# Two column chunks of the composed weights change their widths: 384, 512 becomes 512, 384

## The chip, the cores and the metric

The kernel runs on one core of a Trainium2 chip. The metric is the device time of one execution in microseconds (us). Three runs of the kernel before gave 673.21, 673.73 and 673.96 us; the median is 673.73 us.

## The reference

An input x of 8 sequences by 256 tokens by 1024 features goes through four residual layers. All shapes are 1024 by 1024.

```python
x = x + x @ w_eff.T                      # layer 0: quantized weight plus lora_B @ lora_A / 2
x = x + x @ W.T + 2 * lora(gates, A, B)  # layer 1: top 2 of 8 experts, gates from the logits x @ Wr.T
x = x + x @ W2.T + b + 2 * (x @ A2[id2]) @ B2[id2]   # layer 2: an adapter for each sequence
x = x + x @ W3[id3].T                    # layer 3: a whole weight for each sequence
```

The quantized weight of layer 0 is worked out from thresholds between the codebook's values, with a scale for every group of 128 inputs.

## The kernel before, in words

Everything is computed in float32 accuracy from two float32r parts: each operand is split into a high part (a copy by ScalarE, ACT) and a low part (whole minus high, by VectorE, DVE), and `product` (L1042) issues three matmuls, L1044, L1045 and L1046, for each pair of tiles.

**First phase: the weights are composed before x is touched.** The layers are linear apart from the gates, so the kernel first forms (I + W0)(I + W1)(I + W2) and the columns of the low-rank parts with it. There are two products ("steps"), each with eight row tiles m (`chunk`, L1083). The right-hand operand of step 0 is `e_both` (W2 transposed with the identity added, then the adapters' columns), and its row tiles of the left-hand operand, from W1, pass through a ring of two buffers, `ring_hi` and `ring_lo`. The results are evacuated by ACT (L582) into `e_mid`, split again (`e1`, L636, L643) and are the right-hand operand of step 1, whose left-hand tiles come from the quantized W0; its results go back to `e_both` (`e2`, L644, L650). The columns of each product are cut in three chunks, `LEFT` in step 0 and `RIGHT` in step 1: chunk 0 is 384 wide, chunk 1 is 512, chunk 2 is 256 or 392. A chunk of one row tile is 24 matmuls (8 tiles of the inner dimension, three each) into one PSUM bank.

**Order of step 0.** `CHUNKS` (L59) begins with chunk 0 of row tiles 0 and 1, then chunk 1 of both, then chunk 2 of both; from row tile 2 on the three chunks of a tile stand together. Behind the first, third and fifth of them stand `br(0)`, `br(1)` and `br(2)` (L1070), 24 matmuls each of the same widths as `LEFT`.

**How W2 arrives.** `load_w2` (L352) loads chunk c in pieces kk of two inner tiles: pieces (c, 0) to (c, 3) for chunks 0 and 1, one piece for chunk 2. Those of chunk 0 are used in the order 2, 3, 1, 0 (`W2_ORDER`); piece 2 is issued from ACT's queue and the others from SyncE's (SP). Where an inner tile k meets its own diagonal block, the identity is added to the raw data: by GpSimd (POOL) at L479, by DVE for k = 1 at L870. `CHUNK_OF` (L43) says which chunk holds the diagonal block of tile k, and `w2_diagonals` (L337) makes the list of a piece. Only then does ACT take the high part of the piece (L558), DVE the low part (L762), and PE may use it (`wait_left`, L1063).

**One list for three engines.** `phase1_plan` (L91) writes one list of steps which ACT, DVE and POOL each walk in order, each doing what is its own. In it stand the pieces of W2, the LoRA deltas (L547), the evacuations `f`, the adapters' columns `as` (L624), the ring tiles `w1` and `w0` (L568), and the "beats", the rounds in which DVE and ACT quantize W0 (L823 to L842, L575). Each engine is blocked by the first step that isn't ready.

**Second phase.** Four groups of 512 tokens: `x3_main`, the gates, the low-rank closing, and the product with the weight of layer 3. In the first group the eight tiles m of `x3_main` read `e_both` in column blocks of 128 and wait at L1153 for the chunks of step 1.

Of the kernel before, what the change touches and what calls it, by code (L numbers as in the profile page):

```python
# [36 lines left out]
TILE_AT = [A0, A0 - R2]  # L37
A_AT, WR_AT, NOW_AT = [0, R2], [ER, R2 + ER], [ER + NE, 0]

LEFT = [(0, 384), (384, 512), (896, 256)]  # L40
RIGHT = [(0, 384), (384, 512), (896, 392)]
assert sum(LEFT[2]) == A0 and sum(RIGHT[2]) == EC
CHUNK_OF = [0, 0, 0, 1, 1, 1, 1, 2]  # L43


W2_ORDER = [(2, 3, 1, 0), (0, 1, 2, 3), (0,)]
# [90 lines left out]
def build(nc, x, cb, lang, id2, id3, w0, scale_log, lora_a, lora_bt, w1, wrt, at, bcat,  # L137
          w2t, b, las, lbs, w3t, y):
    plan = phase1_plan()
    with ExitStack() as ctx:  # L140
# [191 lines left out]
        def w2_piece(c, kk):  # L332

            c0, w = LEFT[c]
            return slice(2 * kk, KT if c == 2 else 2 * kk + 2), slice(c0, min(c0 + w, D))

        def w2_diagonals(c, kk):  # L337

            return [k for k in range(KT) if CHUNK_OF[k] == c and (c == 2 or k // 2 == kk) and k != DVE_DIAG]

# [196 lines left out]
        def _(act):  # L537
# [40 lines left out]
            def evac(n):  # L578
                step, m, c = CHUNKS[n]
                c0, w = (LEFT, RIGHT)[step][c]  # L580
                act.wait_ge(chunk_mm, n + 1)
# [8 lines left out]
            for item in plan:  # L590
# [24 lines left out]
                elif what == "br":  # L615
                    c0, w = LEFT[item[1]]
                    act.wait_ge(br_mm, item[1] + 1)
# [18 lines left out]
                elif what == "e1":  # L636
                    _, c, kk = item
                    c0, w = RIGHT[c]
                    ks, cols = slice(2 * kk, 2 * kk + 2), slice(c0, min(c0 + w, A0))
# [4 lines left out]
                elif what == "e2":  # L644
                    _, c, kk = item
                    c0, w = RIGHT[c]
                    ks, cols = slice(2 * kk, 2 * kk + 2), slice(c0, c0 + w)
# [103 lines left out]
        def _(dve):  # L751
# [101 lines left out]
            for item in plan:  # L853
# [43 lines left out]
                elif what == "br":  # L897
                    c0, w = LEFT[item[1]]
                    dve.wait_ge(br_up, item[1] + 1)
# [23 lines left out]
                elif what == "e1":  # L923
                    _, c, kk = item
                    c0, w = RIGHT[c]
                    n_e1 += 1
# [3 lines left out]
                elif what == "e2":  # L930
                    _, c, kk = item
                    c0, w = RIGHT[c]
                    n_e2 += 1
# [107 lines left out]
        def _(pe):  # L1041
            def product(out, a, b_, start, stop, **kw):  # L1042

                pe.matmul(out, a[0], b_[0], start=start, stop=False, **kw)  # L1044
                pe.matmul(out, a[0], b_[1], start=False, stop=False, **kw)  # L1045
                return pe.matmul(out, a[1], b_[0], start=False, stop=stop, **kw)  # L1046
# [23 lines left out]
            def br(c):  # L1070
                c0, w = LEFT[c]
                if c == 0:
                    pe.wait_ge(bcat_lo, 1)
                if c < 2:
                    pe.wait_ge(delta_out, BR_BANK[c] + 1)
                if c == 2:
                    pe.wait_ge(br_down, 1)
                for k in range(KT):
                    ins = product(ps[:, BR_BANK[c], 0:w], (bcat_up[:, k, :], bcat_down[:, k, :]),
                                  (e_hi[:, k, c0:c0 + w], e_lo[:, k, c0:c0 + w]), k == 0, k == KT - 1)  # L1080
                ins.then_inc(br_mm, 1)
# [71 lines left out]
            def x3_main(g, m):  # L1153

                if m < 3:
                    pe.wait_ge(y_free, KT * g + 5 + m)
                if m == 3:
                    pe.wait_ge(e2_down, 12)
                if m >= 5:
                    pe.wait_ge(x3_done, KT * g + m - 4)  # L1160
                for k in range(KT):
                    if m == 0 and k % 2 == 0:

                        pe.wait_ge(e2_down, 4 + k // 2 + 1)
                        pe.wait_ge(x_lo_done, X_CREDIT + 4 * g + k // 2 + 1)
                    cols = slice(m * P, (m + 1) * P)
                    ins = product(ps[:, m % 5, :], (e_hi[:, k, cols], e_lo[:, k, cols]),
                                  (x_hi[:, k, :], x_lo[:, k, :]), k == 0, False, skip_group_check=True)
                if m == KT - 1:
                    ins.then_inc(x_used, 1)  # L1170
# [57 lines left out]
            def group(g):  # L1228
                x3_main(g, 0)
                low_rank(g)  # L1230
                x3_main(g, 1)
                x3_main(g, 2)
                turn_h2(g)
                turn_g(g)
                x3_main(g, 3)
                h2_add(g)
                x3_main(g, 4)
                for m in range(3):
                    x3_gate(g, m)
                pe.wait_ge(h2_done, g + 1)  # L1240
                pe.wait_ge(bs_done, BS_CREDIT + 2 * (g + 1))
                for m in range(3):
                    x3_close(g, m)
                for m in range(3, 5):
                    x3_gate(g, m)
                    x3_close(g, m)
                for m in range(5, KT):
                    x3_main(g, m)
                    x3_gate(g, m)
                    x3_close(g, m)  # L1250
                y_product(g, 0)
                y_product(g, 1)
# [44 lines left out]
```

## Time and profile before

| | |
|---|---|
| median of three runs | 673.73 us |
| the profiled execution | 672.66 us |
| its span in the trace | 670.8 us |
| PE busy | 663.7 us (99%) |
| PE weight load busy | 569.2 us (85%) |
| DVE busy | 353.4 us (53%) |
| ACT busy | 279.3 us (42%) |
| POOL busy | 90.7 us (14%) |
| DMA | 67.07 MB, 100 GB/s on the mean |
| chain that ended last | PE 92%, SP queue 3%, DVE 2% |

All times of the trace are counted from the start of the span; 1.9 us of the profiled execution lie outside it. Matmuls overlap, so the distance between two starts, not the duration of one, is what a matmul costs in a row of them.

### The profile page before, as it was taken

To read this page: it belongs to the slowest core of one execution; us is meant where nothing else is said; L and a number is where in the kernel's file an instruction comes from. 1 tells how busy PE (TensorE), PEld (TensorE's weight loads), DVE (VectorE), ACT (ScalarE), POOL (GpSimd) and SP (SyncE) were. 2 spreads that over 40 slices of the span, in tenths; PEclk is the share of its full clock that TensorE was granted. 3 is DMA by queue.
4 is the path that set the end of the run, shared out by engine and by line. 5 is a ranking of instruction groups with operands and counts; after the bars stand their busy time and mean duration, and the time that the engine had idled before them with its cause. 6 is when DMAs were issued, how large, how long until landed. Compare 5 with 4: busy or idle time off the path is not lost.

```text
span 670.8 us, 9252 instructions
## 1 busy us (share of the span) xinstructions
PE 663.7 (99%) x3280; PEld 569.2 (85%) x3280; DVE 353.4 (53%) x538; ACT 279.3 (42%) x417; POOL 90.7 (14%) x120
## 2 busy tenths in 40 slices
PE   7999999999999999999999999999999999999998
PEld 7889989999999988888889888888888888888886
DVE  6799899879951374215544222661421653411453
ACT  6664664952812361204552123553121564121453
POOL 3210225005010030001220000220000221000120
PEclk9999999999999999999999999999999999999999
DMA  9652111001000503003864001777000586000372
GB/s 317 190 158 84 43 38 57 1 1 63 1 1 0 189 21 129 1 1 104 298 220 155 0 0 44 260 239 231 0 0 0 193 286 214 21 0 1 104 233 103
DMA packets 39283, 67.07 MB, mean 100 GB/s; under 512 B 3541, under 2 KB 22997, under 8 KB 39253
## 3 DMA queue, kind: packets, MB, share of 16 engines
q1 hardware_dynamic: 34500, 58.15, 26.5%
q10 hardware_dynamic: 4752, 8.52, 3.7%
q8 instruction: 18, 0.29, 0.2%
q14 instruction: 13, 0.10, 0.1%
HBM read 58.27 MB, written 8.39 MB: 99 GB/s over the span
## 4 chain that ended last, share of the span: by engine, by line
PE 92%; SPq 3%; DVE 2%; DMA 1%; issue 1%; ACT 1%; DVEq 0%; ACTq 0%
PE ps L1044 28%; PE ps L1046 28%; PE ps L1045 28%; PE ps L1147 3%; PE ps L1149 1%; PE ps L1180 1%; SPq L354 1%; DMA ids_sb<-adapter 1%; DVE tmp L833 1%; SPq L394 1%; SPq L395 0%; DVE w_w L823 0%; ACT tmp L575 0%; DVE w_w L829 0%; SPq L359 0%
## 5 line engine op out<-in xcount | busy, mean ns | idle before, releaser
L762 DVE TENSOR_TENSOR ring_lo<-raw,ring_hi 128x512 fp32r<-128x512 f32 x128 | 91.5, 730 | 82.1 <-ACT ring_hi L674 82.0
L1044 PE MATMUL ps<-e_both,ring_hi 128*128 128x384 f32 (+3 forms) x384 | 133.7, 348 | 0.8 <-DVE ring_lo L762 0.4
L1046 PE MATMUL ps<-e_both,ring_lo 128*128 128x384 f32 (+3 forms) x384 | 133.4, 347 | 0.0
L674 ACT ACTIVATE ring_hi<-raw 128x512 fp32r<-128x512 f32 x128 | 79.4, 629 | 70.2 <-PE ps L1046 66.6
L1044 PE MATMUL ps<-x_both,e_both 128*128 128x512 f32 x256 | 101.5, 397 | 0.0
L1045 PE MATMUL ps<-x_both,e_both 128*128 128x512 f32 x256 | 101.2, 395 | 0.0
L1044 PE MATMUL ps<-ring_hi,e_mid 128*128 128x512 f32 x256 | 101.0, 395 | 0.0
L1046 PE MATMUL ps<-ring_hi,e_mid 128*128 128x512 f32 x256 | 101.0, 395 | 0.0
L1045 PE MATMUL ps<-ring_lo,e_mid 128*128 128x512 f32 x256 | 101.0, 394 | 0.0
L1046 PE MATMUL ps<-x_both,e_both 128*128 128x512 f32 x256 | 101.0, 394 | 0.0
L516 POOL TENSOR_TENSOR raw<-raw,ident 128x128 f32<-128x128 f32 x64 | 43.0, 674 | 317.2 <-DMA raw<-w_t 317.2
L1044 PEld LDWEIGHTS ps<-e_both,ring_hi 128*128 128x128 f32 x384 | 72.1, 188 | 6.8 <-DVE e_both L762 0.7
L1046 PEld LDWEIGHTS ps<-e_both,ring_lo 128*128 128x128 f32 x384 | 72.1, 188 | 5.7
L1018 DVE SCALAR_TENSOR_TENSOR e_mid<-ps,bias_col,e_mid 128x512 fp32r<-128x512 f32 x32 | 22.5, 746 | 94.7 <-ACT e_mid L720 94.7
L1045 PE MATMUL ps<-e_mid,ring_hi 128*128 128x384 f32 (+2 forms) x192 | 68.5, 357 | 0.0
L1045 PE MATMUL ps<-e_both,ring_hi 128*128 128x384 f32 (+2 forms) x192 | 64.8, 337 | 0.0
L575 ACT ACTIVATE tmp<-tmp,dif 128x1024 f32<-128x1024 f32 x48 | 54.2, 1151 | 22.2 <-DVE tmp L831 18.4
L833 DVE SCALAR_TENSOR_TENSOR tmp<-w_w,thr,tmp 128x1024 f32<-128x1024 f32 x48 | 60.4, 1301 | 4.2 <-ACT tmp L575 3.8
L720 ACT ACTIVATE e_mid<-ps,bias_col 128x512 fp32r<-128x512 f32 x32 | 20.4, 690 | 96.5 <-PE ps L1180 96.5
L1046 PEld LDWEIGHTS ps<-ring_hi,e_mid 128*128 128x128 f32 x256 | 48.2, 188 | 11.3
L1046 PEld LDWEIGHTS ps<-x_both,e_both 128*128 128x128 f32 x256 | 48.1, 188 | 11.5
L1045 PEld LDWEIGHTS ps<-ring_lo,e_mid 128*128 128x128 f32 x256 | 48.2, 188 | 11.3
(152 smaller groups left out, 860.9 us busy)
## 6 DMA issues: line engine op xcount, KB each, us to landing
raw<-w_t SPq DMA_DIRECT2D x64, 512.0 KB, 3.5
xraw<-x_t SPq DMA_DIRECT2D x16, 512.0 KB, 4.6
w_w<-w SPq DMA_DIRECT2D x15, 512.0 KB, 4.0
y<-tmp ACTq DMA_DIRECT2D x30, 256.0 KB, 2.6
e_both_w<-w_t SPq DMA_DIRECT2D x5, 512.0 KB, 8.4
e_mid_w<-bs SPq DMA_DIRECT2D x24, 64.0 KB, 2.8
e_both_w<-w_t SPq DMA_DIRECT2D x3, 384.0 KB, 6.7
w_w<-w SPq DMA_DIRECT2D x2, 256.0 KB, 5.2
```

Of the source, the lines that this page charges most:

```text
L354: queue.dma_start(e_lo_w[:, ks, cols], w2t[ks.start * P:ks.stop * P, cols].rearrange("(k p) c -> p k c", p=P)).then_inc(s_w2[4 * c + kk], 16)
L516: pool.tensor_tensor(d, d, ident[:, :], ALU.add).then_inc(w3_diag, 1)
L575: act.activation(acc[i], acc[i], ACT.Identity, bias=dif[:, LEVELS - 1 - level:LEVELS - level]).then_inc(q_add, 1)
L674: act.activation(ring_hi[:, (2 * k + h) % 4, :], raw[:, k % RAW, h * 512:(h + 1) * 512], ACT.Copy).then_inc(w3_hi, 1)
L720: act.activation(x3_hi[:, m, :], ps[:, m % 5, :], ACT.Identity, bias=bias_col[:, m:m + 1]).then_inc(x3_hi_done, 1)
L762: return dve.tensor_tensor(out, whole, hi.bitcast(F32), ALU.subtract)
L833: ins = dve.scalar_tensor_tensor(out=acc[i], in0=qf, scalar=thr[:, k:k + 1], in1=acc[i], op0=ALU.is_gt, op1=ALU.mult)
L1018: dve.scalar_tensor_tensor(out=x3_lo[:, m, :], in0=ps[:, m % 5, :], scalar=bias_col[:, m:m + 1], in1=x3_hi[:, m, :].bitcast(F32), op0=ALU.add,
L1044: pe.matmul(out, a[0], b_[0], start=start, stop=False, **kw)
L1045: pe.matmul(out, a[0], b_[1], start=False, stop=False, **kw)
L1046: return pe.matmul(out, a[1], b_[0], start=False, stop=stop, **kw)
L1147: pe.matmul(ps[:, 4 + t, 0:2 * TW].rearrange("p (h c) -> p h c", h=2), x_hi[:, k, cols], e_both[:, :, k, ecols], start=k == 0, stop=False, ...
```

## The change

```diff
-LEFT = [(0, 384), (384, 512), (896, 256)]
-RIGHT = [(0, 384), (384, 512), (896, 392)]
+LEFT = [(0, 512), (512, 384), (896, 256)]
+RIGHT = [(0, 512), (512, 384), (896, 392)]
...
-CHUNK_OF = [0, 0, 0, 1, 1, 1, 1, 2]
+CHUNK_OF = [0, 0, 0, 0, 1, 1, 1, 2]
...
-                if m == 3:
+                if m == 4:
                     pe.wait_ge(e2_down, 12)
```

The first chunk of both products takes 512 columns and the second 384. The diagonal block of inner tile 3 (columns 384 to 511) is now in chunk 0, and with it its identity addition belongs to piece (0, 1). In the second phase the fourth tile of `x3_main` lies wholly in chunk 0, so that the wait for chunk 1 stands before the fifth. The number of instructions on every engine is the same.

POOL's identity additions at the opening, as one piece of the difference (`s_w2_1` is the landing of piece (0, 1), `s_w2_0` of piece (0, 0), `s_w2_5` of piece (1, 1); `e_both_w` is the float32 view of `e_both`):

```order
 L479 TENSOR_TENSOR e_both_w<-e_both_w,ident 128x128 [waits s_w2_1,lora_clear]
+L479 TENSOR_TENSOR e_both_w<-e_both_w,ident 128x128 [waits s_w2_1]
 L479 TENSOR_TENSOR e_both_w<-e_both_w,ident 128x128 [waits s_w2_0]
 L479 TENSOR_TENSOR w_w<-w_w,ident 128x128 [waits s_w1_1]
-L479 TENSOR_TENSOR e_both_w<-e_both_w,ident 128x128 [waits s_w2_5]
```

One addition moved from piece (1, 1) to piece (0, 1), ahead of that of piece (0, 0).

ACT's walk through the pieces of chunk 0, one piece of the difference (`w2_diag` counts POOL's additions):

```order
-L558 ACTIVATE e_both<-e_both_w 128x2x384 [waits s_w2_2]
-L558 ACTIVATE e_both<-e_both_w 128x2x384 [waits s_w2_3]
+L558 ACTIVATE e_both<-e_both_w 128x2x512 [waits s_w2_2]
+L558 ACTIVATE e_both<-e_both_w 128x2x512 [waits s_w2_3]
 L568 ACTIVATE ring_hi<-w_w 128x512 [waits first_diag]
-L558 ACTIVATE e_both<-e_both_w 128x2x384 [waits w2_diag,s_w2_1]
-L558 ACTIVATE e_both<-e_both_w 128x2x384 [waits w2_diag_dve,w2_diag,s_w2_0]
+L558 ACTIVATE e_both<-e_both_w 128x2x512 [waits w2_diag,s_w2_1]
+L558 ACTIVATE e_both<-e_both_w 128x2x512 [waits w2_diag_dve,w2_diag,s_w2_0]
```

The four steps keep their places; each is 1024 elements long instead of 768.

ACT's queue between the second chunk of PE and the adapters' columns, again from the difference (`chunk_mm` is PE's finished chunk, `s_as` the landing of the adapters):

```order
-L582 ACTIVATE e_mid_w<-ps 128x384 [waits chunk_mm]
+L582 ACTIVATE e_mid_w<-ps 128x512 [waits chunk_mm]
 L547 ACTIVATE raw<-ps 128x512 [waits delta_mm] x3
 L558 ACTIVATE e_both<-e_both_w 128x8x128 [waits w2_diag,s_w2_8]
 L624 ACTIVATE e_both<-w_w 128x8x128 [waits s_as]
```

The evacuation of the second chunk (chunk 0 of row tile 1) is wider and nothing else moved; what stands behind it is queued behind PE's end of that chunk.

## Rows read from the trace of the kernel before

**Rows 1.** The page: busy time and the clock granted to PE.
```profile
PE 663.7 (99%) x3280; PEld 569.2 (85%) x3280; DVE 353.4 (53%) x538; ACT 279.3 (42%) x417; POOL 90.7 (14%) x120
...
PEclk9999999999999999999999999999999999999999
```
**Rows 2.** Waits of PE, whole span: us in total, times, longest.
```profile
PE ps L1044 <- DVE ring_lo L762: 0.4, 1, 0.4
PE ps L1044 <- DVE e_both L762: 0.4, 1, 0.4
```
**Rows 3.** Timeline of PE at the opening: start us, duration us, instruction.
```profile
12.66 0.34 PE L1046 MATMUL ps<-e_both,ring_lo 128*128 128x384 f32 x1
13.37 0.45 PE L1044 MATMUL ps<-e_both,ring_hi 128*128 128x384 f32 x1 [0.37 <-DVE e_both L762]
13.65 0.34 PE L1045 MATMUL ps<-e_both,ring_hi 128*128 128x384 f32 x1
...
15.41 0.34 PE L1046 MATMUL ps<-e_both,ring_lo 128*128 128x384 f32 x1
15.80 0.45 PE L1044 MATMUL ps<-e_both,e_mid 128*128 128x384 f32 x1
...
24.30 0.39 PE L1044 MATMUL ps<-e_both,ring_hi 128*128 128x512 f32 x1
...
27.10 0.39 PE L1044 MATMUL ps<-e_both,ring_hi 128*128 128x512 f32 x1
```
**Rows 4.** Timeline of PE where row tile 2 begins.
```profile
49.29 0.28 PE L1045 MATMUL ps<-e_both,ring_hi 128*128 128x256 f32 x1
49.41 0.28 PE L1046 MATMUL ps<-e_both,ring_lo 128*128 128x256 f32 x1
50.11 0.44 PE L1044 MATMUL ps<-e_both,ring_hi 128*128 128x384 f32 x1 [0.42 <-DVE ring_lo L762]
```
**Rows 5.** Timeline of POOL: identity additions of the opening.
```profile
10.11 2.14 POOL L479 TENSOR_TENSOR e_both_w<-e_both_w,ident 128x128 f32<-128x128 f32 x2 [7.55 <-DMA e_both_w<-w_t]
...
21.77 0.46 POOL L479 TENSOR_TENSOR e_both_w<-e_both_w,ident 128x128 f32<-128x128 f32 x1 [0.74 <-DMA e_both_w<-w_t]
```
**Rows 6.** The first two of these additions: ns min/median/max.
```profile
L479 POOL TENSOR_TENSOR e_both_w<-e_both_w,ident x2: 909/1090/1271, 10.1 to 11.3; 128x128 f32<-128x128 f32 x2
```
**Rows 7.** Transfers at the opening: one window, last columns clock, DMA share, GB/s.
```profile
8.00:12.00 4.00, 4.00 (x33) 4.00 (x32) 3.45 (x6) 2.89 (x5) 1.89 (x2) 1.00 1.07 388
```
**Rows 8.** Timeline of ACT.
```profile
11.47 0.85 ACT L558 ACTIVATE e_both<-e_both_w 128x768 fp32r<-128x768 f32 x1 [0.62 <-POOL e_both_w L479]
...
24.53 0.49 ACT L582 ACTIVATE e_mid_w<-ps 128x384 f32<-128x384 f32 x1
24.91 1.57 ACT L547 ACTIVATE raw<-ps 128x512 f32<-128x512 f32 x3
26.35 1.08 ACT L558 ACTIVATE e_both<-e_both_w 128x1024 fp32r<-128x1024 f32 x1
31.61 1.06 ACT L624 ACTIVATE e_both<-w_w 128x1024 fp32r<-128x1024 f32 x1 [4.18 <-DMA w_w<-as]
```
**Rows 9.** Timeline of DVE.
```profile
10.10 0.95 DVE L762 TENSOR_TENSOR e_both<-e_both_w,e_both 128x768 fp32r<-128x768 f32 x1
10.97 0.95 DVE L762 TENSOR_TENSOR ring_lo<-w_w,ring_hi 128x512 fp32r<-128x512 f32 x1
...
14.34 1.41 DVE L762 TENSOR_TENSOR e_mid<-e_mid_w,e_mid 128x1024 fp32r<-128x1024 f32 x1
...
29.34 1.21 DVE L762 TENSOR_TENSOR e_both<-e_both_w,e_both 128x1024 fp32r<-128x1024 f32 x1
32.70 1.23 DVE L762 TENSOR_TENSOR e_both<-w_w,e_both 128x1024 fp32r<-128x1024 f32 x1 [2.15 <-ACT e_both L624]
```
**Rows 10.** Timeline of ACT at the end of step 1.
```profile
236.76 2.32 ACT L650 ACTIVATE e_both<-e_both_w 128x768 fp32r<-128x768 f32 x3 [0.51 <-PE ps L1046]
...
242.34 2.96 ACT L650 ACTIVATE e_both<-e_both_w 128x1024 fp32r<-128x1024 f32 x3 [1.95 <-PE ps L1046]
```

## The prediction
> **What bounds the kernel now.** I read the page first: PE is busy in 99% of the span at a clock that is granted in full in every slice [rows 1]. So only two things can change the time: the matmuls themselves, and the few moments in which PE has none. Next, the waits of PE over the whole span: two lie before the first chunk and read nothing that the change touches. The other two, 0.4 us each [rows 2], are a piece of W2 that is late at 13.37 us and the ring tile that is late at 50.11 us. The timeline of PE shows what each costs between starts. One 384-wide matmul takes 0.176 us in a row of them (13.65 to 15.41, ten steps), one 512-wide matmul 0.233 us (24.30 to 27.10, twelve steps) [rows 3]. From 12.66 to 13.37 PE loses 0.71 - 0.18 = 0.53 us, and 0.11 us more because the first matmul after a stop is 0.28 us from the second. Before `br(0)` it loses 0.21 + 0.11 = 0.32 us [rows 3], and at row tile 2, where a 256-wide matmul costs 0.12 us, 0.70 - 0.12 + 0.11 = 0.69 us [rows 4]. After 50.11 us PE waits for nothing, so whatever delay it has there stays to the end.
>
> **What the change costs on PE itself: nothing.** Per column the two widths cost the same (0.176/384 = 0.46 ns, 0.233/512 = 0.46 ns), and the products hold 24 matmuls of each width wherever they did before. What is added in chunk 0, 24 x (0.233 - 0.176) = 1.4 us for each row tile, is taken away again in chunk 1. The same holds for the evacuations and splits of ACT and DVE, for the bytes of W2 and for POOL's eight additions: sums are unchanged, only the time of each moves. It is the opening that is sensitive to that.
>
> **The piece (0, 1), step by step.** PE needs the pieces in the order 2, 3, 1, 0, and stands at the third of them now. The chain to it is: landing, POOL's addition, ACT's high part, DVE's low part.
> - Landing. POOL sat idle until the piece landed at 10.11 us [rows 5]. Pieces 2, 3 and 1 grow by 128 KB each, 393 KB in all, ahead of that moment. The queues run at 388 GB/s here [rows 7], which makes +1.0 us. Bounds: nothing, if something other than bytes sets the landing; 1.2 us if the rate is a fifth lower.
> - A second addition. Inner tile 3 now belongs to this piece, so POOL has two to do before ACT may start. The two additions at 10.11 took 1.27 and 0.91 us [rows 6], while one that ran with DVE idle took 0.46 us [rows 5]. I take the median, +1.1 us, because DVE will be in the same run of splits; the bounds are 0.46 and 1.27.
> - ACT's part grows from 0.85 us to 1.06 (a 1024-element one), +0.2 us [rows 8]. DVE's part grows from 0.95 to 1.21, +0.25 us [rows 9].
>
> Sum: the piece is ready 2.55 us later, at 13.37 + 2.55 = 15.9 us. In front of it, pieces 2 and 3 keep PE busy 12 x 0.057 = 0.7 us longer; the first of them may come a few tenths later as well, but PE then stands waiting for piece (0, 1) in any case, so that costs nothing of its own. Behind it come 12 matmuls at 0.233 = 2.8 us, with 0.11 for the stop: `br(0)` begins at 18.83. The B columns' low part, for which PE loses 0.32 us now, is ready in time: DVE follows with piece (0, 0) and then 1.41 us for it [rows 9], 15.9 + 1.15 + 1.4 = 18.45. Today `br(0)` begins at 15.80, in effect 15.91. The difference is 2.92 us, of which 1.4 is only work drawn forward. PE's net loss is **1.5 us**.
>
> **Does the wait at 50.11 us swallow it?** It could take up to 0.69 us, if the ring tile came at its old time. Its chain goes back over the beats to the adapters' split on ACT, which today waits 4.18 us for its transfer and starts at 31.61 [rows 8]. In ACT's queue four steps stand before it, the first of which waits for PE's second chunk. That chunk ends after three groups that each grow by 1.4 us (chunk 0, `br(0)`, chunk 0 of row tile 1), and 1.5 us late besides: 24.53 + 4.2 + 1.5 = 30.25. Then 0.5 for the evacuation, 1.44 for three deltas (24.91 to 26.35) and the 1.08 us split [rows 8]: 33.3. DVE takes 1.15 us for the low part of that split and begins that of the adapters at 34.4, where it begins at 32.70 today [rows 9]. So the cover of 4.2 us is used up, and the beats, which nearly fill DVE until then, start 1.7 us late. The ring tile comes at 50.1 + 1.7, PE arrives at 49.53 + 1.5 = 51.0 and still waits. Nothing is swallowed; the later of the two chains counts: **+1.7 us**.
>
> **Later boundaries: costed at nothing.** In steady state the evacuation of a tile stands behind a ring split that already waits for that whole tile. At the end of step 1, ACT's steps are released by PE at 236.76 (chunk 0 done) and 242.34 (chunk 1 done) [rows 10]. With chunk 0 wider the first becomes 238.2 and the second remains, both relative to PE. The first pair of inner tiles is ready 1.06 + 1.21 us later, at 240.5, and x3_main begins at 242.3. The cover shrinks from about 3.6 to 1.8 us but holds. The last chunk to be split gets narrower, which only helps. At the end of step 0 the third chunk lies between as well and the cover is larger still.
>
> **Sum.** 672.66 + 1.7 = 674.4 us for an execution like the profiled one. It lay 1.07 us under the median of the runs; on the median, 673.73 + 1.7 = **675.4 us**, +0.25%. About 0.2%, 1.35 us, is what a measurement can tell from no change. The result hangs on one number: the time T at which piece (0, 1) is ready, total = T - 14.2 us. It can be told from no change for T above 15.55.
>
> **Rivals.**
> 1. *Only one DVE operation stands between POOL's two additions and their end (34%).* In the rows the additions end shortly after DVE's two-input operations do: DVE ends at 11.05 and 11.92 [rows 9], POOL at 11.38 and 12.25 [rows 5, 6]. If that is a mechanism, the second addition does not cost a mean, but a place in DVE's sequence. If the piece lands while DVE is in the low part of piece (0, 2), which ends at about 11.1, the first addition gets through at 11.4 and the second after DVE's next operation, at about 12.8. Then T = 12.9 + 1.06 + 1.21 = 15.2 and the total is **+1.0 us, 674.7**. If it lands just after, each addition has an operation of DVE before it, ends come to about 13.7, T to 16.0, total +1.8. Landing and DVE's boundary both fall near 11.1 and I can't order them; that the landing is late by full bytes speaks for the second. By the Trainium skill, "SBUF — State Buffer", section "SBUF: two separate sides", a DVE operation with two SBUF inputs and a GpSimd operation exclude each other on a shared port pair, and the loser blocks for the other's whole instruction. By that rule the trace agrees: 0.46 us alone, 0.91 to 1.27 beside DVE.
> 2. *The opening absorbs it (8%): the other side.* If landings are not set by bytes, T rises only by the second addition, 0.9, and 0.45 for ACT and DVE: T = 14.7, total +0.5 us, 674.2. Without the 0.9 as well PE's loss would vanish, and the 0.53 and 0.32 us that it loses today could turn into a gain of at most 0.8 us, 672.9. It decides for a "no change" wherever T is below 15.55. Against it: the queues are never idle there, at a DMA share over 1 [rows 7].
> 3. *The delay is larger (13%).* Landing 1.2, addition 1.27 each with a further DVE operation between, T = 16.6: +2.4 us, 676.1. The threshold computations and their followers on DVE stand before the adapters too, and would carry this on.
> 4. *A later cover breaks (3%)*, at the start of `x3_main`, if the split of chunk 0 comes over 1.8 us later than worked out: up to a microsecond on top.
>
> **How the numbers follow.** My own case, T near 15.9, has 42%. The forecast is its time, 675.4. The range takes in rivals 1 and 2 without the gain, and the upper bound of rival 3: 674.2 to 676.3. Slower by over 0.2%: most of my case (0.38), rivals 3 and 4 (0.15) and a few of rival 1 with the scatter of the runs (0.07), 0.6. Faster by over 0.2% would need more than all that PE loses at these two points, 0.04. The rest, 0.36, is within 0.2%.
>
> **What would show it.** In the changed profile: a wait of PE for the low part of `e_both` of about 2 us, ending near 15.9; POOL's first three additions in one run from about 11.1 us; no stop before `br(0)`, near 18.8; the adapters' split on ACT without a wait for the transfer, near 33.2; the wait for `ring_lo` still there, ending near 51.8; no new wait after. A ring wait that is gone, or a third wait of PE after 52 us, would show the working wrong, and so would POOL starting at 10.1.

## The result and the profile after

Over 22 runs of each kernel on the same chips the changed kernel has a median of 674.27 us and the kernel before 673.56. The ratio is 1.0013 with a 95% interval of 1.0007 to 1.0019: it is slower, by 0.9 us (0.5 to 1.3). One run of the changed kernel, 723.33 us at a granted clock of 0.85, is left out of the ratio; the other 21 lie within 673.48 to 676.73. The forecast was 675.4 in 674.2 to 676.3. Direction and range hold, the range by 0.07 us; the size of 1.7 us is about twice what was measured. Of the prediction's three cases the one with 0.36, a change within 0.2%, came true, and not "slower by over 0.2%", to which it gave 0.6. The profiled execution took 673.80 us, its span is 672.0 (before 672.66 and 670.8): 1.14 us more.

The page of the changed kernel, as in [rows 1]: the same numbers of instructions, PE busy for 0.8 us more, and a first slice of the clock that is no longer a 9.

```profile
PE 664.5 (99%) x3280; PEld 570.7 (85%) x3280; DVE 354.1 (53%) x538; ACT 279.0 (42%) x417; POOL 86.3 (13%) x120
...
PEclk8999999999999999999999999999999999999999
```

All waits of PE in the changed kernel, beside [rows 2], which leave out the two ahead of the first chunk:

```profile
PE ps L1057 <- DVE bc_hi L762: 2.4, 1, 2.4
PE ps L1119 <- POOL br_now_lo L473: 1.6, 1, 1.6
PE ps L1044 <- DVE ring_lo L762: 0.2, 1, 0.2
```

The wait at the ring tile is there, smaller than foretold, and nothing follows it. The wait of 2 us for piece (0, 1) is not there. In its place PE waited a microsecond longer before its first LoRA product (L1057): 2.4 us instead of 1.4. The timeline of PE shows both ends of chunk 0, `br(0)`, and row tile 2, as in [rows 3, 4]:

```profile
12.91 0.40 PE L1044 MATMUL ps<-e_both,ring_hi 128*128 128x512 f32 x1
...
15.46 0.40 PE L1046 MATMUL ps<-e_both,ring_lo 128*128 128x512 f32 x1
15.74 0.50 PE L1044 MATMUL ps<-e_both,ring_hi 128*128 128x512 f32 x1
16.08 0.40 PE L1045 MATMUL ps<-e_both,ring_hi 128*128 128x512 f32 x1
...
18.63 0.39 PE L1044 MATMUL ps<-e_both,e_mid 128*128 128x512 f32 x1
...
51.22 0.50 PE L1044 MATMUL ps<-e_both,ring_hi 128*128 128x512 f32 x1 [0.18 <-DVE ring_lo L762]
```

Chunk 0 began at 12.91 instead of 10.74, so PE came late enough for piece (0, 1) to be only 0.05 us late (15.74 after 15.46, where 0.23 is a step). With the 0.11 us of the stop PE lost 0.16 us at the piece. Without any loss there `br(0)` would have begun at 12.91 + 24 x 0.233 = 18.50 instead of 18.63: in this execution PE's own late start and the late piece come to nearly the same time. The piece was ready at 15.7 (foretold 15.9), `br(0)` began at 18.63 (18.83), row tile 2 at 51.22 (51.8). The times are nearly those of the working; what stands behind them is not, as the rows of the three engines that prepare the piece show. ACT, DVE and POOL, in this order:

```profile
9.29 2.01 ACT L558 ACTIVATE e_both<-e_both_w 128x1024 fp32r<-128x1024 f32 x2 [0.43 <-DMA e_both_w<-w_t]
12.11 0.63 ACT L568 ACTIVATE ring_hi<-w_w 128x512 fp32r<-128x512 f32 x1 [0.81 <-DVE w_w L865]
12.64 1.04 ACT L558 ACTIVATE e_both<-e_both_w 128x1024 fp32r<-128x1024 f32 x1
```

```profile
10.38 1.23 DVE L762 TENSOR_TENSOR e_both<-e_both_w,e_both 128x1024 fp32r<-128x1024 f32 x1 [1.23 <-ACT e_both L558]
11.52 0.55 DVE L865 TENSOR_TENSOR w_w<-w_w,ident 128x128 f32<-128x128 f32 x1
11.99 1.48 DVE L762 TENSOR_TENSOR e_both<-e_both_w,e_both 128x1024 fp32r<-128x1024 f32 x1
13.40 0.95 DVE L762 TENSOR_TENSOR ring_lo<-w_w,ring_hi 128x512 fp32r<-128x512 f32 x1
14.27 0.28 DVE L870 TENSOR_TENSOR e_both_w<-e_both_w,ident 128x128 f32<-128x128 f32 x1
14.47 2.61 DVE L762 TENSOR_TENSOR e_both<-e_both_w,e_both 128x1024 fp32r<-128x1024 f32 x2
```

```profile
11.27 1.13 POOL L479 TENSOR_TENSOR e_both_w<-e_both_w,ident 128x128 f32<-128x128 f32 x2 [8.71 <-DMA e_both_w<-w_t]
```

The landing came at 11.27, 1.16 us later than in [rows 5] (foretold 1.0). POOL's two additions took 1.13 us together, 0.57 each, and were done at 12.40; ACT was busy with its ring step until 12.7 and started on the piece without a wait. DVE is the engine that had no gap: from 10.38 on its operations stand end to end, and the low part of piece (0, 1) is the sixth of them. It started at 10.38 because ACT had waited for the landing of piece (0, 2) until 9.29. So the path to the piece was the landing of (0, 2), ACT's 1.06, and DVE's queue.

DVE's queue had no gap in the kernel before either, and the prediction's rows left out the lines that say so:

```profile
9.03 0.96 DVE L762 TENSOR_TENSOR e_both<-e_both_w,e_both 128x768 fp32r<-128x768 f32 x1 [0.55 <-ACT e_both L558]
9.90 0.28 DVE L865 TENSOR_TENSOR w_w<-w_w,ident 128x128 f32<-128x128 f32 x1
...
11.85 0.55 DVE L870 TENSOR_TENSOR e_both_w<-e_both_w,ident 128x128 f32<-128x128 f32 x1
12.36 1.99 DVE L762 TENSOR_TENSOR e_both<-e_both_w,e_both 128x768 fp32r<-128x768 f32 x2
```

DVE ended its own identity addition at 12.40 and ACT the high part of the piece at 12.32 ([rows 8], 11.47 + 0.85): two paths to one time, of which the prediction followed the one over POOL and ACT. From these rows the delay adds up as follows. DVE's queue starts 1.35 us later (10.38 after 9.03), its stretch up to the piece is 0.76 us longer (4.09 instead of 3.33), and the piece's own low part 0.25 (1.21 instead of 0.96): 2.36 us, and 13.37 + 2.36 = 15.7.

From there to row tile 2 the chain is as told. ACT's step for the adapters' columns, then DVE's for them and DVE's for the ring tile (compare [rows 8, 9]):

```profile
32.84 1.08 ACT L624 ACTIVATE e_both<-w_w 128x1024 fp32r<-128x1024 f32 x1
```

```profile
34.14 1.22 DVE L762 TENSOR_TENSOR e_both<-w_w,e_both 128x1024 fp32r<-128x1024 f32 x1
...
49.94 1.22 DVE L762 TENSOR_TENSOR ring_lo<-w_w,ring_hi 128x1024 fp32r<-128x1024 f32 x1
```

The cover of the adapters' transfer is used up, and DVE starts on them at 34.14 instead of 32.70, +1.44 (foretold 34.4, +1.7). The ring tile comes at 49.94. Before it stood here:

```profile
48.84 1.22 DVE L762 TENSOR_TENSOR ring_lo<-w_w,ring_hi 128x1024 fp32r<-128x1024 f32 x1
```

That is only +1.10, since between the two lie the split of `br(1)`, which is now 384 wide (0.55 us instead of 0.68 on DVE), and a pair of quantizing operations that took 2.48 us instead of 2.69.

Two theories went to the chip. **A** is the working of the prediction: bytes and POOL's second addition make the piece late, PE loses net time before `br(0)`, and the beat chain carries at least as much to row tile 2. **D** is what the profile after says: DVE's own queue behind the late first landing makes the piece late, the second addition lies beside it. A rival **C** puts the loss in the late first products: the 32 LoRA products of PE ahead of chunk 0. Ratios below are to the kernel before, run on the same chip.

### The profile page after: what moved, and what is told of

Its sections match the earlier page's. It is cut to its first block, busy times and chain, and to the rows that moved or that the text cites. A ratio compares the mean times of both kernels' runs of the same rounds, so it can differ in the third digit from the quotient of the medians.

```text
span 672.0 us, 9251 instructions
## 1 busy us (share of the span) xinstructions
PE 664.5 (99%) x3280; PEld 570.7 (85%) x3280; DVE 354.1 (53%) x538; ACT 279.0 (42%) x417; POOL 86.3 (13%) x120
## 4 chain that ended last, share of the span: by engine, by line
PE 95%; DVE 3%; ACT 1%; DMA 1%; issue 0%; ACTq 0%; DVEq 0%
PE ps L1044 29%; PE ps L1046 29%; PE ps L1045 29%; PE ps L1147 3%; PE ps L1149 1%; PE ps L1180 1%; DVE tmp L833 1%; PE ps L1057 1%; DMA xraw<-lora_b_t 1%; PE ps L1059 1%; DVE w_w L823 0%; ACT tmp L575 0%; DVE w_w L829 0%; DVE e_both L762 0%; PE ps L1196 0%; PE ps L1188 0%
## 5 line engine op out<-in xcount | busy, mean ns | idle before, releaser
L1044 PE MATMUL ps<-e_both,ring_hi 128*128 128x512 f32 (+3 forms) x384 | 133.6, 348 | 0.2 <-DVE ring_lo L762 0.2
L1046 PE MATMUL ps<-e_both,ring_lo 128*128 128x512 f32 (+3 forms) x384 | 133.4, 347 | 0.0
L1045 PE MATMUL ps<-e_mid,ring_hi 128*128 128x512 f32 (+2 forms) x192 | 68.6, 357 | 0.0
L1045 PE MATMUL ps<-e_both,ring_hi 128*128 128x512 f32 (+2 forms) x192 | 64.8, 337 | 0.0
```

## Experiments

### Only the left product's widths

The changed kernel, with the widths of the right product as before:

```diff
-RIGHT = [(0, 512), (512, 384), (896, 392)]
+RIGHT = [(0, 384), (384, 512), (896, 392)]
...
-                if m == 4:
+                if m == 3:
                     pe.wait_ge(e2_down, 12)
```

> The widths of step 0 (LEFT, CHUNK_OF) as in the changed kernel, those of step 1 (RIGHT) and the wait of x3_main as before. Theory A (all of the loss is made in the opening, where only the left product's widths act): as the changed kernel, +0.7 to +1.2 us over the kernel before, and the end of step 1 shows no wait of PE either way. Rival (a part of it is lost at the hand-over between the steps or to the second phase): below +0.4 us, or a new wait of PE near 130 or 242 us.

674.35 us, ratio 1.0012 (1.0003 to 1.0021), the same as the change (1.0013). No wait of PE after row tile 2. The loss is made by step 0's widths, as far as this interval can tell, and the second product's widths, the hand-over and the start of `x3_main` cost nothing that can be seen. In its profile chunk 0 began at 13.20 and no piece was late: `br(0)` began at 18.76, where 13.20 + 24 x 0.233 gives 18.79.

### The identity of tile 3 on DVE

```diff
-DVE_DIAG = 1
+DVE_DIAG = 3
```

> The changed kernel with DVE, not POOL, adding the identity of inner tile 3 (and POOL that of tile 1): piece (0, 1) has one addition on each engine. Theory A as it was predicted (POOL's second addition costs about 1.1 us on the path): piece (0, 1) is ready about 1 us earlier, total 0.5 to 1.1 us below the changed kernel. Theory D, from the changed profile, where ACT began piece (0, 1) straight behind its ring step and DVE had no gap (DVE's own queue, started by the late landing of piece (0, 2), is the path): ready within 0.3 us of the changed kernel, total within 0.3 us of it.

675.30 us, ratio 1.0023 (1.0014 to 1.0033): 0.7 us above the change by the ratios, where A wanted 0.5 to 1.1 below it. D was wrong about the size as well, since it expected no difference: it had not reckoned that ACT must now wait for DVE's addition, which stands behind everything in DVE's queue. ACT in this kernel:

```profile
14.76 1.06 ACT L558 ACTIVATE e_both<-e_both_w 128x1024 fp32r<-128x1024 f32 x1 [1.93 <-DVE e_both_w L870]
```

It began the piece at 14.76 instead of 12.64, and PE came to it at 17.13. What is put on DVE there is on the path. In this execution chunk 0 also began late, at 13.98, so that the piece alone cost PE 0.5 us.

### The identity of tile 3 left out

```diff
-            return [k for k in range(KT) if CHUNK_OF[k] == c and (c == 2 or k // 2 == kk) and k != DVE_DIAG]
+            return [k for k in range(KT) if CHUNK_OF[k] == c and (c == 2 or k // 2 == kk) and k not in (DVE_DIAG, 3)]
```

> The changed kernel without the identity addition of inner tile 3 (the identity is left out of that one diagonal block). Theory A as predicted (the second addition is about 1.1 us of the path): 0.6 to 1.1 us below the changed kernel, the level of the kernel before. Theory D (the addition lies beside DVE's own queue): within 0.3 us of the changed kernel, +0.5 to +1.1 us over the kernel before.

674.08 us, ratio 1.0007 (0.9998 to 1.0016): below the change by 0.2 us by the medians and 0.4 by the ratios. The times can't tell D's bound (0.3 us) from A's (0.6 to 1.1). The profile can. ACT again starts on the piece straight behind its ring step, at the same distance from it:

```profile
11.77 0.63 ACT L568 ACTIVATE ring_hi<-w_w 128x512 fp32r<-128x512 f32 x1 [0.81 <-DVE w_w L865]
12.31 1.05 ACT L558 ACTIVATE e_both<-e_both_w 128x1024 fp32r<-128x1024 f32 x1
```

So ACT never waited for the second addition. It has a smaller price, which neither theory named: it holds DVE. The low part of piece (0, 3), which took 1.48 us beside it, takes 1.21 without it:

```profile
11.66 1.21 DVE L762 TENSOR_TENSOR e_both<-e_both_w,e_both 128x1024 fp32r<-128x1024 f32 x1
```

DVE's stretch from its start to the piece is 3.83 us (10.05 to 13.88) instead of 4.09. That `br(0)` begins at 18.68 as in the change (18.63) says nothing about the piece: chunk 0 began at 13.11 here, and 24 steps from there give 18.70.

### Both kernels once more: a second profile of each opening

> The changed kernel again, for a second profile of its opening. Theory A and D: the first product may start anywhere from 10.7 to 13 us, according to when the LoRA transfers land and whether the clock granted falls to 0.5 for a while, but piece (0, 1) is ready at 15.2 to 16.0 us and the ring tile of row tile 2 at 50.9 to 51.6 in every execution. Rival C (the late start of the first products and the lower clock make the loss): with a start near 10.7 us the total is that of the kernel before.

673.78 us; chunk 0 from 12.85, `br(0)` at 18.63, row tile 2 at 51.21: to 0.1 us the first profile again, as A and D expected of it. It doesn't speak against C, since its first products were late too.

> The kernel before again, for a second profile of its opening. Theories A and D: ring tile 2 within 0.3 us of 50.1, and piece (0, 1) used at 13.2 to 13.6 us. Rival C (the clock's fall is a thing of single executions that costs): where the clock falls here, the span is 0.5 us or more longer.

674.15 us, and here is the surprise of the study. The kernel before, profiled a second time, shows an opening quite unlike the one that the prediction was worked out on. Its PE:

```profile
7.49 0.55 PE L1057 MATMUL ps<-bc_lo,bc_hi 128*128 128x256 f32 x1 [2.11 <-DVE bc_hi L762]
...
8.91 0.41 PE L1057 MATMUL ps<-bc_lo,bc_hi 128*128 128x256 f32 x1
9.12 0.41 PE L1059 MATMUL ps<-x_pair,bc_hi 128*128 128x256 f32 x1
...
13.88 0.34 PE L1044 MATMUL ps<-e_both,ring_hi 128*128 128x384 f32 x1
...
18.07 0.34 PE L1044 MATMUL ps<-e_both,e_mid 128*128 128x384 f32 x1
...
51.71 0.34 PE L1044 MATMUL ps<-e_both,ring_hi 128*128 128x384 f32 x1
```

The first LoRA product starts 0.65 us later, and then 25 of the 32 take a step of 0.21 us instead of 0.12. Chunk 0 begins at 13.88 instead of 10.74. PE never waits for W2 afterwards, nor for the ring: it gets to row tile 2 at 51.71, 1.6 us later than in the profile on record, and the span is 1.5 us longer (672.3 against 670.8). The ring tile itself came at its time (DVE's step for it began at 49.15 after 48.84), as A and D had it, but their second number, PE at piece (0, 1) by 13.6, did not hold: PE had not even begun chunk 0. For this kernel C's expectation is the one that came true in substance, a slow pace and over 0.5 us more, although the granted clock of the profile reads 1.00 there. The kernel before has two limits here, PE's late start and the ring tile, and which one counts differs between executions.

### Ring tile 2 one beat earlier, in both kernels

```diff
-    plan += some(2) + [("br", 1)] + some(1) + [("f", 3)] + some(1) + [("w1", 2), ("f", 4)] + some(2) + [("br", 2)]
+    plan += some(2) + [("br", 1)] + some(1) + [("f", 3), ("w1", 2)] + some(1) + [("f", 4)] + some(2) + [("br", 2)]
```

> The kernel before, with ring tile 2 of W1 split one beat earlier in the plan (in front of the beat after evacuation 3). Theory A (the loss at row tile 2 is the beat chain, not PE's arrival): the wait at 50.1 us goes; where the opening is early PE arrives at 49.5 us and the time falls by 0.4 to 0.7 us; where the opening is late (first product at 13.9 us, as in the second profile of before) nothing is gained. Median 0.1 to 0.6 us below before. Rival (a new wait on ACT takes its place): unchanged or slower.

> The same move in the changed kernel. Its PE arrives at 50.9 us and waits until 51.2: 0.3 to 0.4 us below the changed kernel, so +0.4 to +0.7 us over the kernel before, and still slower than before_ring by 0.8 to 1.3 us, PE's own net loss. If the beat chain alone made the loss, after_ring would be level with before_ring within 0.3 us.

In the kernel before: 672.74 us, ratio 0.9990 (0.9981 to 1.0000), 0.7 us less; in the changed one 673.74, ratio 1.0006 (0.9998 to 1.0015). Neither waits at row tile 2 any more in its profile, where PE begins it at 50.29 and 50.81. Between the two medians there is still 1.0 us, so the beat chain alone was not the loss: PE itself arrives later. The profile of after_ring shows another way through the opening: piece (0, 1) landed only at 12.29, ACT waited 1.9 us for it and for POOL's two additions (0.88 us together), and `br(0)` still began at 18.56. In such an execution the second addition, some 0.4 us, would be on the path; that is argued from the rows, no run without the addition landed so late. Of the runs of before_ring two, 674.35 and 674.53, gained nothing, as would be if their opening was late.

### More bytes ahead of the pieces, and the new cut of the transfers alone

The first adds three transfers of 128 KB to the kernel before:

```diff
+            sp.dma_start(tmp[:, 1, 0:256], w2t[0:P, 256:512]).then_inc(s_extra, 16)
             load_w2(sp, 0, W2_ORDER[0][1])
...
+            sp.dma_start(tmp[:, 2, 0:256], w2t[0:P, 512:768]).then_inc(s_extra, 16)
             for kk in W2_ORDER[0][2:]:
                 load_w2(sp, 0, kk)
...
             load_w2(act, 0, W2_ORDER[0][0])
+            act.dma_start(tmp[:, 0, 0:256], w2t[0:P, 0:256]).then_inc(s_extra, 16)
...
                 elif what == "thr":
+                    dve.wait_ge(s_extra, 48)
                     thresholds()
```

> The kernel before with three extra transfers of 128 KB into a buffer that is free, queued like the growth of the first three pieces of chunk 0 (one behind piece (0, 2) on ACT's queue, two on SP's ahead of pieces (0, 3) and (0, 1)); DVE waits for them before the thresholds. Nothing of it is used. Theory A: it is the bytes that make the pieces late: POOL is released for piece (0, 1) at 10.8 to 11.4 us instead of 9.7 to 10.1, and PE is 0 to 0.5 us later at row tile 2 (the wider splits are missing). Rival (bytes are no matter): POOL released at 9.7 to 10.3 us, time as before.

675.14 us, ratio 1.0029 (1.0019 to 1.0038), well beyond what was expected. POOL was released for the piece at 12.58, where 10.8 to 11.4 had been expected, and PE then waited at row tile 2 (lines are 4 or 5 higher in this kernel):

```profile
PE ps L1049 <- DVE ring_lo L766: 1.6, 1, 1.6
```

This is a badly chosen test. Unlike the change, it lengthens the whole queue, so that everything behind, the adapters included, comes later too. It shows that the time grows with more bytes in the queue, and that is all; the landing at 12.58 is a single one, and the changed kernel had one at 12.29 (after_ring) without them. The second is the cleaner one, since the sum of bytes stays:

```diff
-            ks, cols = w2_piece(c, kk)
+            ks, _ = w2_piece(c, kk)
+            cols = (slice(0, 512), slice(512, 896), slice(896, D))[c]
```

> The kernel before, except that the transfers of W2 have the new cut (columns 0 to 511, 512 to 895, 896 to 1023); the splits, additions and products keep 384, 512, 256. Theory A (the bytes ahead of the pieces make most of the loss): POOL released for piece (0, 1) at 11.0 to 11.5 us, as in the changed kernel, and a time 0.4 to 1.0 us over the kernel before. Rival (the longer splits and the wider chunk make it): released there too, but within 0.3 us of the kernel before.

673.62 us, ratio 1.0003 (0.9994 to 1.0012): no change. POOL was released by the landing at 11.16:

```profile
11.16 2.13 POOL L480 TENSOR_TENSOR e_both_w<-e_both_w,ident 128x128 f32<-128x128 f32 x2 [8.60 <-DMA e_both_w<-w_t]
```

So the landing does move by the microsecond that bytes make. More than one pair of profiles says it: in the eight with the new cut of the transfers POOL was released for the piece at 10.58 to 12.29 us, 11.18 on the mean, in the five with the old cut and no added bytes at 9.73 to 10.51, 10.15 on the mean.

The piece moved with it. DVE came to its low part at 13.39 instead of 12.36, 1.03 us later, and caught nothing up. PE didn't notice, because it began chunk 0 only at 13.21 in this execution, and 12 steps of 0.176 us from there are 15.3. A's expectation of 0.4 to 1.0 us is not borne out, but the interval reaches 0.8 us and so does not exclude it. No run had the longer splits without the later landings, so how the loss divides between the two is not shown.

### Twelve warm-up products instead of eight, and both edits together

```diff
-WARM_UP = 8
+WARM_UP = 12
```

> The kernel before with 12 instead of 8 warm-up products, so that PE is busy until about 7.3 us and the stretch without work before the first LoRA product goes. Theory C2 (in a part of the executions the LoRA products start late and run at a granted clock of 0.5, so that chunk 0 starts at 13 to 14 us and PE, not the beat chain, arrives last at row tile 2): the granted clock stays at 1.0 there, chunk 0 starts by 12 us in all executions, and the median falls by 0.3 to 1.0 us with a narrower spread. Rival (the clock's fall lies beside the path): no change.

673.34 us, ratio 0.9994 (0.9985 to 1.0003), 0.4 us less by the ratio and 0.1 by the medians: it is unclear whether anything was gained. Its profile says why: chunk 0 now began at 11.04, 30 of the 32 LoRA products ran at the 0.12 us step, but the adapters came late in this execution and PE waited 1.3 us for ring tile 2. With one limit gone the other one holds. C2's clock and start came as expected; its gain can't be told, and the runs are not narrower (672.51 to 674.25).

> The kernel before with both edits, ring tile 2 one beat earlier and 12 warm-up products. Where the opening was late in before_ring (674.4 and 674.5 us) the clock is now kept, and the wait at row tile 2 that before_warm12 still had (1.3 us in its profile) is gone: 0.9 to 1.3 us below the kernel before, all runs within 1 us. Rival (the two limits are one and the same): no better than before_ring, -0.7 us.

> The changed kernel with both edits. What is left against before_ring_w12 is the net loss of PE in front of br(0) alone. Theory A: 1.0 to 1.6 us over before_ring_w12 (1.5 predicted, less where the pieces land early), so 0 to +0.5 us over the kernel before. If the loss were made by late first products and the fallen clock, it would be level with before_ring_w12.

The kernel before with both edits: 672.40 us, ratio 0.9985 (0.9976 to 0.9994), eleven runs within 671.91 to 672.90. It is the fastest version of the study, 1.1 us below the kernel before. Its first LoRA products, at full pace:

```profile
7.37 0.36 PE L1057 MATMUL ps<-bc_lo,bc_hi 128*128 128x256 f32 x1 [0.79 <-DVE bc_hi L762]
7.56 0.28 PE L1059 MATMUL ps<-x_pair,bc_hi 128*128 128x256 f32 x1
7.68 0.28 PE L1057 MATMUL ps<-bc_lo,bc_hi 128*128 128x256 f32 x1
```

The changed kernel with both edits: 673.69, ratio 1.0007 (0.9998 to 1.0016). The distance between the two, 1.3 us by the medians, is the price of the new widths where the first products run at full pace and the ring tile is early. The wait that the prediction had foretold appears in this one, where chunk 0 began at 11.66:

```profile
15.44 0.50 PE L1044 MATMUL ps<-e_both,ring_hi 128*128 128x512 f32 x1 [0.54 <-DVE e_both L762]
```

The piece is late behind DVE's queue again, which runs from 10.09 to it without a gap. Here it started so late because ACT began piece (0, 2) at 9.01 straight behind its LoRA delta, not because of a landing. The two profiles put 0.77 us between the starts of `br(0)` net of the 1.4 us of columns (18.34 - 16.17 - 1.4), and 0.7 between those of row tile 2 (50.55 and 49.87). Of the 0.77 us, 0.39 is a later start of chunk 0 (11.66 after 11.27); the rest is lost at the pieces. The medians' 1.3 us is more than that pair of executions shows: the profiled one of the changed kernel, 673.03 us, was the fastest of its eleven, and of those up to 675.4 no profile was taken.

## Why the prediction came out as it did

- **The place was right.** Nothing but the opening matters: putting the widths of step 1 back changed nothing that can be seen (left_only), no later wait appeared, and columns, evacuations and bytes kept their sums. The costing at nothing of the later boundaries holds.
- **The landing, +1.0 us: right.** 11.18 us against 10.15 on the mean of the profiles. What the prediction waved aside, that the first piece "may come a few tenths later as well, but ... costs nothing of its own", did matter: ACT started piece (0, 2) at 9.29, released by its landing, where it had started it at 8.15 before, and DVE's whole queue hangs on it. In the second profile of the changed kernel the start is the same (9.28). In three others (after_noadd, after_dvediag, after_ring_w12) ACT came to the piece straight behind its LoRA delta, at 8.97, 9.39 and 9.01, so there the late start is that of PE's first products.
- **The second addition, +1.1 us: this step failed.** It was put on the path at the median of two additions that had DVE beside them. The two took 1.13 us together and ended before ACT was free; the second cost 0.26 us of DVE's queue, by holding DVE (after_noadd). That T still came out at 15.7 was luck: the term stood in for DVE's queue, in which longer low parts (1.23 and 1.48 us where 0.96 and 0.95 stood) follow a start that is 1.35 us later (10.38 against 9.03). Nor does the total follow from T as the prediction has it: T - 14.2 gives 1.5 us, and the two profiles differ by 1.14.
- **Rival 1 was right in that the place in DVE's sequence decides, not a mean**, and its +1.0 us is nearest to the 0.9 measured; as a time, rival 2's 674.2 lies nearer to 674.27, but its condition, landings that bytes don't move, did not hold. Rival 1's own mechanism did not set the end. POOL got its additions through, and here it was DVE that was held: the additions of 128x128 on DVE took 0.55 instead of 0.28, the low part beside POOL 1.48 instead of 1.21. By the Trainium skill, "SBUF — State Buffer", section "SBUF: two separate sides", whichever of the two starts first keeps the shared ports; the trace agrees, in both directions.
- **PE's net loss, 1.5 us: nearly right against the profile it was worked out on, for another reason, and too much for the median.** Against that profile `br(0)` is 18.63 - 1.40 - 15.91 = 1.3 us later. But PE lost only 0.16 us at the late piece, less than the 0.64 and 0.32 that the kernel before lost at its two stops. What made it late is its own start of chunk 0 at 12.91 instead of 10.74, which the prediction didn't have. The profiles show why the two hide each other. With the wide first chunk `br(0)` began within 18.34 to 18.76 in six of seven profiles, 16.9 to 17.4 net of the columns, whether chunk 0 began at 11.66 (1.1 us lost at the pieces, after_ring_w12) or at 13.20 (nothing lost, left_only); the seventh is after_dvediag. With the narrow one and the old transfers it began at 15.80 to 16.65 in four profiles and at 18.07 in the fifth, the second profile of before, which lost nothing to waits for W2, since its first products were late anyway. So the medians differ by less than the two first profiles do (0.7 or 0.9 against 1.14), most likely because the changed kernel's opening takes the place of a delay that the kernel before has in part of its executions. With twelve warm-up products and the early ring tile the difference is 1.3 us, but the intervals of the two ratios are too wide to call that growth shown.
- **"Nothing is swallowed": right in kind.** DVE began the adapters 1.44 us later. The chain behind gave 0.34 us back, so that 1.10 us arrived at row tile 2: 0.13 by `br(1)`, now narrower, which stands in it and which the working had left out, and 0.21 by the quantizing pair. The pair's cause is open; with the widths of step 0 alone (left_only) it took 2.69 us as before. With the ring tile early in both kernels, the loss stays.
- **Rival C** as the only cause is out: with first products at full pace the changed kernel is still 1.3 us slower by the medians. That late first products cover part of the loss is what the profiles suggest.

Still open: how often each kernel's executions begin late. Profiles are single executions, and each was one draw. Open too is whether the larger transfers make the late start likelier: PE's first LoRA product began at 6.84 us in one of eight profiles with the new cut of the transfers (7.39 to 7.82 in the others) and in three of five with the old one (7.37 and 7.49 in the others). No run tested it.

## What to carry to other kernels

When a piece of data grows, don't follow only the engine that gets a new operation; walk every in-order queue from the first landing on, and look for the one without a gap. In the profile before, DVE's rows showed it already. A forecast below a microsecond needs more than one profiled execution of the kernel before, since a second limit may cover the first in some of them. And a start that looks the same in two profiles (`br(0)` at 18.63 and 18.68) shows an edit to be without effect only if the same limit set it in both.

## What the runs showed of the hardware that was not expected

- The 32 LoRA products behind the warm-up ran at a step of 0.12 us throughout only in the first profile of the kernel before and with twelve warm-up products (two of three profiles, the third but for two). In the ten other profiles, with eight warm-up products and waits of 1.4 to 2.4 us ahead, 15 to 25 of them took 0.21 us. The length of the wait does not decide it by itself: PE had waited 1.45 us in the first profile of before, and 1.45 us in that of before_ring, where 16 products were slow. The granted clock tells of it only in a part: these are the windows from 8 to 12 us of the changed kernel and of the second profile of before, where the column reads 0.57 and 1.00, although PE issued only 23 and 21 matmuls in them against 33 in [rows 7].

```profile
8.00:12.00 4.00, 4.00 (x23) 4.00 (x23) 2.74 (x5) 2.60 (x3) 0.73 (x2) 0.57 1.08 404
```

```profile
8.00:12.00 4.00, 4.00 (x21) 4.00 (x20) 3.01 (x5) 2.52 (x4) 1.11 (x2) 1.00 1.07 389
```

So the pace of the matmuls has to be read beside the clock. From 9 to 11 us the column of the changed kernel reads 0.50, which is TensorE's lower level of 1.2 GHz. In the five profiles where it fell (after, left_only, loads_only, after_noadd, after_ring) PE had done nothing for 1.8 to 2.4 us and then issued 5 to 10 products at full pace; in the five where the pace fell and the column stayed at 1.00 the products were slow from the first on.
- Moving 393 KB ahead of a piece within a full queue delayed its landing by 1.0 us on the mean (11.18 us in eight profiles against 10.15 in five), as much as the 388 GB/s of [rows 7] give; single landings scatter over 1.7 us (10.58 to 12.29).
- An addition of 128x128 on POOL and a DVE operation with two inputs beside it lengthen each other: POOL's takes 0.46 us alone and up to 1.27 beside DVE, DVE's own addition 0.28 and 0.55, its low part of 1024 elements 1.21 and 1.48.
